# Attention output turned by VectorE in 32x32 blocks, and routing computed inside batch 0

## What is computed

```
xn = layernorm(x)
q, k, v = xn @ Wq, xn @ Wk, xn @ Wv          # 16 heads of 8
q, k = l2norm(q), l2norm(k)                  # per head
attn = softmax(causal(q @ k.T * 8))          # per batch and head, 512 x 512
attention = concat(attn @ v) @ Wo
probs = softmax(xn @ Wr.T)                   # 8 experts
top_v, top_i = top_k(probs, 2); top_v /= sum(top_v)
ffn = sum over e of w_e * (gelu(xn @ W1[e].T + b1[e]) @ W2[e].T + b2[e])
out = x + attention + ffn
```

## Time and profile before

| | us |
|---|---|
| median of 3 runs | 798.49 (796.7 to 802.25) |
| the profiled execution | 802.14 |
| its span, first to last instruction | 800.4 |
| mean granted clock of TensorE | 0.949 |

### The profile page before, as it was taken

How to read it: one execution, slowest core, us unless ns; L and a number is a source line. 1 busy time by engine, 2 the same in 40 slices (tenths; PEclk the granted TensorE clock), 3 DMA queues, 4 the chain that set the end, 5 groups by cost and what they waited for, 6 DMA issues and landing times. The chain is left out here.

```text
span 800.4 us, 19383 instructions
## 1 busy us (share of the span) xinstructions
PE 716.7 (90%) x6151; PEld 447.5 (56%) x6151; DVE 491.1 (61%) x1318; ACT 495.4 (62%) x833; POOL 431.9 (54%) x558
## 2 busy tenths in 40 slices
PE   2777659999999998999979999999989999999986
PEld 2555512333333334999969999999953333333333
DVE  7799795566556754444424444667645766677743
ACT  2566537788887875444424444444457888887873
POOL 4444417666666667576620016476525666666672
PEclk9888859999999998999989999999989999999998
DMA  7665548443354236644422224344414544444331
GB/s 207 211 211 177 171 113 192 82 85 76 92 97 102 66 83 142 204 143 126 141 66 66 72 79 112 99 117 112 111 39 80 70 96 101 100 113 116 65 93 34
DMA packets 170117, 89.20 MB, mean 111 GB/s; under 512 B 77104, under 2 KB 159824, under 8 KB 170064
## 3 DMA queue, kind: packets, MB, share of 16 engines
q1 hardware_dynamic: 161872, 71.74, 36.4%
q0 software_dynamic: 8192, 16.79, 7.3%
HBM read 39.47 MB, written 32.24 MB: 90 GB/s over the span
## 5 line engine op out<-in xcount | busy, mean ns | idle before, releaser
L674 ACT ACTIVATE prob<-psum 128x1024 f32<-128x1024 f32 x320 | 311.0, 1034 | 89.1 <-PE psum L770 83.8
L686 ACT ACTIVATE prob<-psum,prob 128x256 f32<-128x256 f32 x284 | 117.6, 471 | 157.6 <-PE psum L934 156.7
L795 PE MATMUL psum<-prob,v 128*18 128x384 f32 (+2 forms) x2560 | 180.5, 390 | 2.0 <-POOL prob L564 1.0
L557 POOL TENSOR_SCALAR_AFFINE_SELECT prob<-prob 128x512 f32<-128x512 f32 x128 | 88.1, 688 | 134.2 <-ACT prob L674 133.9
L546 POOL DMA_INDIRECT slot_x<-rows,idx x128 | 126.1, 985 | 48.8 <-issue 29.5
L544 POOL DMA_INDIRECT rows<-slot_y,idx x128 | 123.2, 963 | 53.5 <-issue 25.7
L770 PE MATMUL psum<-qks 32*128 32x512 f16 (+3 forms) x1024 | 126.3, 307 | 23.8 <-ACT prob L674 17.7
L946 PEld LDWEIGHTS psum<-prob 128*128 128x128 f32 x1136 | 138.4, 192 | 3.7
L934 PE MATMUL psum<-xs,prob 128*128 128x256 f32 x568 | 138.8, 388 | 0.0
L946 PE MATMUL psum<-prob 128*128 128x128 f32 x1136 | 138.5, 275 | 0.0
L770 PEld LDWEIGHTS psum<-qks 32*128 32x128 f16 x1024 | 33.9, 92 | 162.7 <-ACT prob L674 105.5
(11 more groups left out here) (146 smaller groups left out, 744.5 us busy)
## 6 DMA issues: line engine op xcount, KB each, us to landing
xs<-slot_x SPq DMA_DIRECT2D x71, 128.0 KB
slot_y<-xs SPq DMA_DIRECT2D x71, 128.0 KB
xs<-in_L_attn_x SPq DMA_DIRECT2D x16, 256.0 KB, 3.3
prob<-in_L_ffn_W SPq DMA_DIRECT2D x16, 256.0 KB, 3.1
xn_rows<-xns SPq DMA_DIRECT2D x16, 256.0 KB, 3.5
xn_cols<-xts SPq DMA_DIRECT2D x16, 256.0 KB, 3.5
xt<-xn_cols SPq DMA_DIRECT2D x16, 256.0 KB, 3.5
rows<-xn_rows SPq DMA_DIRECT2D x16, 256.0 KB, 3.2
```

Of the source, the lines that this page charges most:

```text
L557: pool.affine_select(out=p, in_=p, compare_op=ALU.is_ge, fill=0.0, base=0, pattern=[[0, 2], [0, 2], [1, P]], channel_multiplier=-1).then_i ...
L674: act.activation(prob[:, q % 2, KEPT[u], :], score[(q + u) % 2], ACT.Exp, scale=SCALE / UP ** 2).then_inc(exp_done, 1)
L686: act.activation(hs[:, s, c, :], psum[:, 2 * s + c // 2, (c % 2) * FT:(c % 2 + 1) * FT], ACT.Gelu, bias=ws[:, s, B1C + c:B1C + c + 1]).the ...
L795: mm = pe.matmul(ps_o[32 * g:32 * g + VW, first:first + cols], lhs, prob[:, w % 2, KEPT[u], c:c + cols], start=(i == 0 and not odd), stop= ...
```

## The change

Two changes are made together.

- **Output of attention.** The heads of a half batch gather in banks `ps_o` and `ps_pc` in turn (`ps_octet`). VectorE turns the bank in 32x32 blocks into SBUF, takes the reciprocals, divides into a second tile, and turns that in 32x32 blocks into `ot[half]`; heads lie on partitions 32 g + 9 j. The copy on ScalarE, both kinds of turn on TensorE and the copy L1269 are gone. The out projection adds two halves with Wo padded to those partitions (16 small loads of 8 rows each, after a memset), so 8 matmuls, 16 passes; it stands at w=2, after the products of that step and ahead of the last scores, instead of at w=3. `divide(2b)` comes after `add_attention`.
- **Routing.** All four tiles of batch 0 are prepared before the last selection, and SyncE issues their transposes before it waits for the stores of xn and the norms. Counting, places and ranks move into batch 0: `count_tokens` in w=0 and `place_tokens` at its end on TensorE; on VectorE `segments` at w=1 (which makes `last_i`), `places` at w=2, `find_slots` at w=3, `pick_tiles` at w=0 of batch 1. GpSimd's scatters of batches 0, 1 and 2, 24 in all, stand in batches 1 and 2, 12 in each.

The diff, cut to its core:

```
-            sp.dma_start(wo[:], Wo).then_inc(wv_in, 16)
...
-            sp.wait_ge(zero_made, 1)
+            sp.wait_ge(zero_made, 3)
+            for k in range(H):
+                half, g, j = k // (2 * QH), k // 2 % QH, k % 2
+                r = 32 * g + (DH + 1) * j
+                sp.dma_start(wo[r:r + DH, half, :], Wo[DH * k:DH * (k + 1), :]).then_inc(wo_in, 16)
...
+            for s in range(2):
+                for par in range(2):
+                    sp.wait_ge(cols_out[par][s], 16 * (NB // 4))
+                sp.wait_ge(rows_out[s], 16 * (NB // 2))
+            load_xt(1)
+            sp.wait_ge(norms_ready, NB)
+            load_rows(0, 0)
+            load_rows(1, 1)
             sp.wait_ge(zeroed, 16)
             sp.wait_ge(lasts_ready, 1)
...
-                        if known(b, 0) and slot == 3:
+                        if known(b, 1) and slot == 0:
                             pool.wait_ge(routed, 1)
                             pool.wait_ge(padded, 16 * E)
-                        order = [0], [1], [2], [3], [4], [5], [6], [7]
+                        order = [(b, par, slot)]
                         if known(b, 0):
-                            order = [], [], [], [0, 1], [2, 3], [4, 5], [6], [7]
+                            order = []
+                        if known(b, 1) or known(b, 2):
+                            first = 3 * MOVES // 2 * (b - 1) + 3 * slot // 2
+                            order = [(k // MOVES, k // MOVES % 2, k % MOVES)
+                                     for k in range(first, first + 3 * (slot + 1) // 2 - 3 * slot // 2)]
                         if last:
-                            order = [0, 1], [2, 3], [4, 5], [6, 7], [], [], [], []
-                        for o in order[slot]:
-                            move(b, par, o, second)
+                            order = [(b, par, o) for o in range(2 * slot, 2 * slot + 2)] if slot < MOVES // 2 else []
+                        for m, j, o in order:
+                            move(m, j, o, second)
...
-                        if not odd and some(2 * b + w // 2):
-                            pe.wait_ge(o_evac, 2 * b + w // 2)
+                        if not odd and some(2 * b + w // 2 - 1):
+                            pe.wait_ge(o_evac, 2 * b + w // 2 - 1)
...
             def out_project(b, projected):
-                pe.wait_ge(ot_ready, b + 1)
+                pe.wait_ge(ot_ready, 2 * b + 2)
                 pe.wait_ge(proj_evac, projected)
                 for t in range(TB):
-                    mm = pe.matmul(ps_pa[:, t * D:(t + 1) * D], ot[:, t * P:(t + 1) * P], wo[:],
-                                   start=True, stop=True)
+                    for half in range(2):
+                        mm = pe.matmul(ps_pa[:, t * D:(t + 1) * D], ot[half][:, t * P:(t + 1) * P], wo[:, half, :],
+                                       start=(half == 0), stop=(half == 1))
                 mm.then_inc(outp_done, 1)
...
+            def count_tokens():
+                pe.wait_ge(bt_ready, 1)
+                pe.wait_ge(selected, T // ST)
...
+            def place_tokens():
+                pe.wait_ge(totals_read, 1)
+                pe.wait_ge(later_ready, 1)
...
                     scores(b, par, w, 0)
-                    if w == 1 and not known(b, 0):
-                        if some(2 * b - 1):
-                            pe.wait_ge(norm_done, 2 * b - 1)
-                        turn_o(2 * b - 1)
-                    elif w == 3:
-                        if some(2 * b):
-                            pe.wait_ge(norm_done, 2 * b)
-                        if some(b):
-                            pe.wait_ge(ot_ready, b)
-                        else:
-                            pe.wait_ge(plan_ready, 1)
-                        turn_o(2 * b)
-                    if known(b, 0) and w == 1:
+                    if known(b, 0) and w == 3:
+                        pe.wait_ge(ranks_read, 2)
+                    if known(b, 1) and w == 2:
                         pe.wait_ge(pick_ready, 1)
-                        pe.matmul(ps_pc[:, 0:FFN_TILES], pick[:], identh[:, 0:FFN_TILES], start=True, stop=True)\
-                            .then_inc(picked, 1)
+                        pe.wait_ge(proj_evac, TB * (b + 1) + 2)
+                        pe.matmul(ps_pick, pick[:], identh[:, 0:FFN_TILES], start=True, stop=True).then_inc(picked, 1)
                     scores(b, par, w, 1)
                     if weighs:
                         if w == 1:
                             pe.wait_ge(proj_evac, TB * (b + 1))
                             if known(b, 0):
-                                pe.wait_ge(routed, 1)
+                                pe.wait_ge(cleared, 1)
                         weigh(*before_this, [0])
                     scores(b, par, w, 2)
+                    if known(b, 0) and w == 0:
+                        count_tokens()
                     if weighs:
                         weigh(*before_this, [1, 2])
                     if not last:
                         if w == 1:
+                            if known(b, 0):
+                                pe.wait_ge(counts_read, 1)
                             project(b + 1, 1)
                         elif w == 2:
+                            if known(b, 1):
+                                pe.wait_ge(plan_ready, 1)
                             project(b + 1, 3)
-                    if w == 3 and not known(b, 0):
-                        out_project(b - 1, TB * (b + 1) if last else TB * (b + 2))
                     scores(b, par, w, 3)
                     if weighs:
                         weigh(*before_this, [3, 4])
-                    if w == 1 and not known(b, 0):
-                        turn_on(b - 1)
+                    if w == 2 and not known(b, 0):
+                        if known(b, 1):
+                            pe.wait_ge(wo_in, 16 * H)
+                        out_project(b - 1, TB * (b + 1) if last else TB * (b + 2))
                     scores(b, par, w, 4)
                     if not last:
                         if w == 0:
                             project(b + 1, 0)
+                            if known(b, 0):
+                                place_tokens()
                         elif w == 1:
...
-            prepare(0, 0, 0)
-            prepare(0, 0, 1)
+            for t in range(TB):
+                prepare(0, 0, t)
             for c in range(TOPK):
                 select(T // ST - 1, c)
             dve.wait_ge(btr_done, 1)
             dve.tensor_copy(wexp[:, :, B1C:W2C], psum[:, 6, 0:E * MC].rearrange("p (e c) -> p e c", e=E))\
                 .then_inc(bt_ready, 1)
             dve.wait_ge(counted, 1)
-            dve.tensor_copy(totals.rearrange("p c n -> p (c n)"), ps_o).then_inc(totals_read, 1)
-            for t in range(2, TB):
-                prepare(0, 0, t)
-            dve.wait_ge(counted, 2)
+            dve.tensor_copy(totals.rearrange("p c n -> p (c n)"), ps_count).then_inc(totals_read, 1)
+            dve.memset(ps_o, 0.0).then_inc(cleared, 1)
...
+            def segments():
+                dve.wait_ge(counted, 2)
+                dve.tensor_copy(counts[:], ps_count[:, 0:2 * E].rearrange("p (c e) -> p c e", c=2)).then_inc(counts_read, 1)
+                dve.wait_ge(counts_read, 1)
...
+            by_block = by_token.rearrange("p (j r) -> p j r", r=32)
+            to_block = divided.rearrange("p (j r) -> p j r", r=32)
+            def heads_of(ap):
+                return ap[:, :, 0:VW].rearrange("p j (x y) -> p j x y", x=2)[:, :, :, 0:DH]
+            def divide(k, half, projected):
+                dve.wait_ge(pv_done, 2 * k + 2)
                 if some(k):
                     dve.wait_ge(norm_done, k)
-                dve.reciprocal(rs[:], o[:, :, :, DH:VW:DH + 1]).then_inc(rs_done, 1)
+                dve.transpose(by_token, ps_octet[half]).then_inc(o_evac, 1)
+                dve.wait_ge(o_evac, k + 1)
+                dve.reciprocal(rs[:], by_block[:, :, DH:VW:DH + 1]).then_inc(rs_done, 1)
                 dve.wait_ge(rs_done, k + 1)
-                to = on.rearrange("p t (h c j d) -> p t h c j d", h=2, c=QH, j=2)[:, :, half]
-                dve.tensor_tensor(to, o[:, :, :, 0:VW].rearrange("p t c (j y) -> p t c j y", j=2)[:, :, :, :, 0:DH],
-                                  rs[:].rearrange("p t c (j a) -> p t c j a", a=1).broadcast_to([P, TB, QH, 2, DH]),
+                if some(k):
+                    dve.wait_ge(ot_ready, k)
+                dve.tensor_tensor(heads_of(to_block), heads_of(by_block),
+                                  rs[:].rearrange("p j (x a) -> p j x a", a=1).broadcast_to([P, N // 32, 2, DH]),
                                   ALU.mult).then_inc(norm_done, 1)
+                dve.wait_ge(norm_done, k + 1)
+                if some(projected):
+                    dve.wait_ge(outp_done, projected)
+                dve.transpose(ot[half], divided).then_inc(ot_ready, 1)
...
```

(77 more changed lines are left out.)

168 lines of the change are left out of this document (73 added, 95 removed).

## The result

The changed kernel takes **819.19 us** (816.49 to 821.98, 4 runs) against 798.52 for the kernel before (796.7 to 802.25, 4 runs): a ratio of 1.0253, 95% interval 1.0218 to 1.0289. The profiled execution took 821.98 us, its span is 820.2 us, at a mean granted clock of 0.941 (before: span 800.4, 0.949). So the sign was right. The time lies inside the range given for 8 in 10 (795 to 821) and outside the forecast's own (803 to 816): the size, +20.7 us, is nearly twice the +10.7 forecast.

The account below looks back on a forecast made before the run. TensorE, busy 90% and in lock step with ScalarE, bounds the kernel. Start +5.5, batch 1 +1.3, steady batches -0.3 x 6 and +0.95 x 6, rest: +10.7 on 798.49 gives 809.2 us; range 803 to 816, 8 in 10 795 to 821.

Parts of the forecast that it names:

- Start of batch 1: SyncE's queue: transposes stand behind zero fills, which wait for last_i, and the acc load; batch 1 starts at 141, 5.5 us later.
- queue without the shift: Rival: batch 1 starts where it does now, transposes passing while acc loads; steady waits stay; 803.7 us, chance 0.15.
- dear transposes: Rival: VectorE's 32x32 transposes need two passes, 1.36 us each; 15 us over twelve steady batches, 824 us; chance 0.14 (and between).
- Batch 1: Batch 1 takes 27.6 us against 26.25, +1.3: 24.05 plus 2.6 for the low clock and 0.9 for choosing tiles.
- Steady batches without the wait: TensorE in steady batches: turns removed, projection 16 passes; 24.05 us instead of 24.35, 0.3 less a batch.
- The wait for v in the second half: Batches 9 to 14: out projection at w=2 waits 1.25 us for VectorE's fourth v copy; batches 25.3 us, +0.95 each.
- whose bank it needs free: Out projection at w=2: its bank is free only once VectorE has copied v of the fourth tile; wait 1.25 us.
- so its chain arrives in time even with +0.2, and the wait there is about nothing: First half, steady batches: VectorE's chain to the fourth v copy, 0.2 us longer, causes about no wait; 24.05 us, -0.3.
- the division: VectorE's division reads SBUF instead of PSUM: kept at 0.42 us, nothing added, 0.3 kept for the range.
- Batch 8: The first batch after the experts, 27.0 us before and partly at the low clock, gains 0.3 us.
- Batch 15: The last batch of attention gains 0.2 us.
- Tail and between: Tail after the last product: -1.2 to +0.7, taken +0.5 us; between halves, the division's 1.4 us delay is covered, 0.

Follow-up runs that it names:

- run 3: Changed kernel with the 2 MB load of acc issued ahead of SyncE's wait for last_i, not behind the zero fills: 902.70 us, ratio 1.0153 to the kernel before.
- run 9: Changed kernel, out projection still at w=2 but waiting for the third tile's v copy instead of the fourth's: 803.75 us against 799.10 for the kernel before.
- run 6: Changed kernel with GpSimd's eight indirect transfers per batch only at w=0 and w=3, in batches 3 to 7 and 8 to 14: 867.03 us, ratio 1.087.
- run 10: run 9 plus acc load and batch 1's first transpose ahead of the last_i wait, other transposes between zero fills: 792.73 us, ratio 0.9916 to the kernel before.
- run 12: Kernel before with only the output change, out projection waiting for the third tile's v copy; routing and queue as before: 796.24 us, ratio 0.9971.

## Why the prediction was right in sign and half in size

**Start of batch 1: the mechanism right, the number in part by luck.** First score 102.31 (forecast 101.3), end of last_i 116.08 (114.4), batch 1 at 140.80 (141), +5.31 (+5.5). So last_i came 1.7 us later than forecast, and what stands between it and batch 1 took 24.7 us instead of 26.6; the two errors cancel. The mechanism, transposes issued slowly behind the load of acc, is shown by run 3. The forecast rival "queue without the shift" is out, and so is "dear transposes": they took 0.71 us. That 819 lies near that rival's numbers, 821 and 824, is chance.

**Batch 1: mis-sized.** 26.5 us by the cut of the earlier trace rows (26.08 to its last score group), against 27.6. Ahead of the small product for picking the tiles TensorE waited 0.68 us (forecast 0.9, for pick_ready), but the profile puts it down to a copy of v; the out projection waited another 0.35. Over a batch of 23.86 that leaves about 1.6 us for the low clock (granted clock 0.90), not the 2.6 taken from batch 8.

**Steady batches without the wait: better than forecast.** 23.86 in run 9 against 24.05. The removed turns gave what was forecast, 1.45 us against 1.4 (the one at w=3 0.3: 1.51 us from 685.56 to 687.07 instead of 1.81). The rest is the projection: 16 passes took 1.98 us to the next score (683.58 to 685.56 in run 9), not the 2.18 of two times 1.09.

**The wait for v in the second half: right.** 1.08 us against 1.25. The transposes took 0.707 us from PSUM and 0.711 from SBUF, against 0.72; all 64 lie between 0.70 and 0.72. The estimate of 1.24 us from the Trainium skill ("VectorE: DVE Perf Modes", section "The three transpose paths") doesn't hold for 128x512 in fp32: at 0.71 us its fixed part doesn't recur in every 128 columns. Of the reason given for the wait, "whose bank it needs free", run 9 shows the half that was wrong: the bank was free.

**The step that failed: "so its chain arrives in time even with +0.2, and the wait there is about nothing".** Batches 2 to 6 waited 1.02, 2.35, 0.54, 0.58 and 0.55 us; only batch 7 didn't. The term that was mis-sized is the division, taken at 0.42 from the division of before, with 0.3 kept for the range. In the kernel before all 32 took 0.42 or 0.43, whatever GpSimd did. Of the 32 after, those at w=3 took mostly 0.51 and those at w=1, the ones in the chain, up to 0.87, mean 0.64 over both. With GpSimd idle beside it the new form takes 0.43, so it is not dear by itself. What differs is the second SBUF input, where the earlier trace rows had shown 0.74 for such an instruction. The Trainium skill, "SBUF — State Buffer", section "Who interferes with whom", says that a VectorE instruction with at most one SBUF input doesn't contend with GpSimd, outside its two-port modes, and one with two does, with a GpSimd instruction that reads SBUF; the divisions of run 6 agree, which take the longer the more of a mask is still ahead of them, and so do the transposes with their one input, which never varied. The 0.45 us by which the division at w=1 was short are most of the 0.55. That share is worked out from rows and tested by no run: other instructions of the same chain vary too (a cast 0.28 or 0.72, a product with two SBUF inputs 0.42 or 0.87). In the second half the division was as dear, and the wait still came out under the forecast, because the product behind the projection at w=1 (L1101) took 0.42 there, where it took 0.85 before.

**The term that was missing: what a long wait does to TensorE.** In the profile after, waits of 2.35 and 2.57 us were followed by the low clock (0.59 over the next 3.5 us and 0.51 over the next 9.76). The first came in batch 3, where two products of VectorE (L1100 and L1101) took 0.89 and 1.44 us instead of 0.42, beside GpSimd's masks and scatters; the second in a batch where VectorE's casts and combines, too, ran longer beside GpSimd. That batch and the one after took 26.50 and 28.79 us, 5.3 more than two of 25.0. Shown by run 9: with the wait gone, the granted clock is 1.00 from 605 to 790 us, and batches 8 to 15 take 191.8 us instead of 206.3. Run 6 shows it from the other side, 6.9 us for a wait of 2.27.

**The second half, term by term.** Its +9.47 has three parts. The six stretches from the projection of batch 8 to that of batch 14 came to +9.2 (forecast +5.7): 3.9 for six of 25.0 us, and the 5.3. Batch 8 took 25.0 us against 26.97, -2.0 (forecast -0.3). Batch 15, to its last score group, gave about +2.3 (forecast -0.2); TensorE pauses 1.25 us there for a mask of GpSimd, and the granted clock is 0.50 over the 5.5 us from there. That these two cancel is luck. The same pause stands in run 9, where no low clock follows; the changed kernel, then run 9:

```profile
795.57 2.08 PE L799 MATMUL psum<-prob,v 128*18 128x128 f32 x16 [1.25 <-POOL prob L574]
```
```profile
776.73 0.41 PE L799 MATMUL psum<-prob,v 128*18 128x128 f32 x8 [1.24 <-POOL prob L574]
```

Why the clock falls after this pause in some executions and not in others stays open.

**Tail and between:** 0.0 and +0.56, against +0.5 and 0.

What was left out (the waits of the first half, 5.0 us, and the falls of the clock) was more than what was put too high (batch 1 by 1.0, batch 8 by 1.7, the steady base by 0.2 a batch), hence the factor of two.

## What to carry to other kernels

When a step is moved next to a semaphore count, write down which buffer the count protects, and wait for that buffer's last user, not for the last of the group. A wait on the path can have a price beyond its length, because the clock may fall behind it, so the range must hold that case. And before a blocking wait on a DMA queue, ask what behind it doesn't depend on the waited thing: the load of acc and the first transpose didn't.

## What the runs showed of the hardware

- A 32x32 block transpose of 128x512 in fp32 on VectorE takes 0.71 us from PSUM and from SBUF, beside masks or transfers.
- The division, a product of 256 columns, takes 0.42 or 0.43 us with one SBUF input. With two it takes 0.43 with GpSimd idle or beside an indirect transfer alone, 0.43 to 0.82 when it starts within a mask (the earlier in the mask, the longer), and 0.85 to 0.87 when it starts in a transfer with a mask 0.55 to 0.61 us behind it.
- DMA transposes issue at 1.3 to 1.4 us each with the 2 MB load well ahead of them (runs 3 and 10). Directly behind that load the first takes 7.02 us (7.20 in the kernel before) and the three after it 1.5 each on average.
- A pause of TensorE of 2.3 to 2.6 us was followed by the low clock in each of the places shown, one of 1.1 us in each steady batch mostly not; in run 3 the clock did fall at 752 us, after pauses of 1.06, 1.11 and 1.22 us within 9 us. A pause of 1.24 or 1.25 us in batch 15 was followed by the low clock in the changed kernel and in run 10, and not in runs 9 and 12.
